# Values per tile of 116 tokens, moved to their rows by DMA, in a fused image-and-text transformer kernel

## What is computed

```python
h = concat([tokens(x), txt], axis=1)                 # (64, 87, 256)
y = layernorm(h)
q, k, v = split(y @ w_qkv.T)                         # 16 heads of 16
q, k = rope(norm_per_head(q)), rope(norm_per_head(k))
h = h + (softmax(q @ k.T / 4) @ v) @ w_proj.T + b_proj
z = layernorm(h)
h = h + z @ W_lin.T + b_lin + lora_of_the_top_2_of_8_experts(z)
```

## Time and profile before

| | |
|---|---|
| median of 3 runs | 793.22 us (786.54 to 795.9) |
| the profiled execution's own time | 798.07 us |
| its span, first to last instruction | 796.4 us |
| what lies around the span | 1.7 us |
| mean granted TensorE clock | 0.94 |
| busy: PE, PEld, DVE, ACT, POOL | 708.1, 564.9, 547.5, 408.2, 423.4 us |

### The profile page before, as it was taken

One profiled execution on the slowest core, in us unless ns is written; L12 is line 12 of the kernel. 1 busy time (PEld: TensorE's weight loads), 2 busy tenths in 40 slices (PEclk: granted clock), 3 DMA queues, 4 the chain that ended last, 5 costly groups with the idle time before them and its releaser, 6 DMA issues.

```text
span 796.4 us, 23804 instructions
## 1 busy us (share of the span) xinstructions
PE 708.1 (89%) x9335; PEld 564.9 (71%) x9335; DVE 547.5 (69%) x1208; ACT 408.2 (51%) x985; POOL 423.4 (53%) x450
## 2 busy tenths in 40 slices
PE   5998979987896388999899999999999999999974
PEld 4987757876673266887777777777777777877752
DVE  2377665873877556688677687887887887875641
ACT  4453423623433145666566556656557557666530
POOL 3577442652645726556447457566566566565211
PEclk9999969989897589999999999999999999999995
DMA  9940640704020121211221221222222222121100
GB/s 223 240 110 1 194 131 1 194 17 96 10 58 18 25 53 32 68 49 39 62 73 40 58 70 49 61 67 56 61 61 61 61 52 71 26 52 37 44 19 25
DMA packets 69524, 53.02 MB, mean 67 GB/s; under 512 B 36175, under 2 KB 68646, under 8 KB 69286
## 3 DMA queue, kind: packets, MB, share of 16 engines
q1 hardware_dynamic: 69414, 51.50, 25.9%
HBM read 33.69 MB, written 11.40 MB: 57 GB/s over the span
## 4 chain that ended last, share of the span: by engine, by line
PE 50%; DMA 13%; SPq 12%; DVE 11%; issue 5%; ACT 4%; POOL 4%; DVEq 0%; POOLq 0%; ACTq 0%
DMA out<-out_sb 8%; PE p_c L1305 8%; PE p_a L1305 7%; PE p_conv L764 6%; PE p_kv L764 6%; DMA xcols<-in_x_cols 5%; PE p_s L1366 4%; SPq L1060 4%; SPq L1061 4%; PE p_o L1375 3%; SPq L1050 2%; PE p_n L1383 2%; PE p_c L1423 2%; PE p_s L1348 2%; PE p_mm L764 2%
## 5 line engine op out<-in xcount | busy, mean ns | idle before, releaser
L1100 POOL TENSOR_TENSOR t<-t,ss_rs 116x512 f32<-116x512 f32 x48 | 51.0, 1062 | 152.8 <-ACT ss_rs L1149 152.8
L1243 DVE TENSOR_REDUCE mx<-p_s 87x16 bf16<-87x1392 f32 x64 | 102.2, 1597 | 8.9 <-PE p_s L1348 8.4
L1174 ACT ACTIVATE prT<-p_s 87x1392 f32<-87x1392 f32 x64 | 85.0, 1328 | 31.2 <-PE p_s L1366 31.2
L426 POOL TENSOR_TENSOR xs_lo<-xcols,xs_hi 120x585 fp32r<-120x585 f32 (+1 forms) x45 | 60.5, 1352 | 66.2 <-ACT xs_hi L489 66.2
L1096 POOL TENSOR_TENSOR t<-t 116x512 f32<-116x512 f32 x48 | 61.7, 1285 | 42.0 <-DVE t L1234 41.9
L1366 PE MATMUL p_s<-qr,kr 32*87 32x87 f32 x2048 | 68.6, 257 | 0.0
L1103 POOL TENSOR_TENSOR t<-t,tabs 116x512 f32<-116x512 f32 x48 | 61.1, 1273 | 1.5
L1305 PE MATMUL p_c<-w_f,yT 128*116 128x296 f32 x192 | 59.7, 436 | 1.7 <-ACT f L1199 0.6
L1366 PEld LDWEIGHTS p_s<-qr,kr 32*87 32x87 f32 x2048 | 60.1, 153 | 0.0
L1362 PE MATMUL p_s<-mxT,pick_row 32*87 32x87 bf16 x1024 | 55.7, 207 | 1.0 <-ACT mxT L1168 1.0
L1305 PE MATMUL p_c<-w_p,onT 128*116 128x256 f32 x192 | 54.3, 406 | 1.2 <-ACT yT L1193 0.9
(11 more groups left out here) (248 smaller groups left out, 1974.8 us busy)
## 6 DMA issues: line engine op xcount, KB each, us to landing
xcols<-in_x_cols SPq DMA_DIRECT2D x12, 822.7 KB, 11.8
h<-h_tokens SPq DMA_DIRECT2D x16, 348.0 KB
out<-out_sb SPq DMA_DIRECT2D x48, 116.0 KB
h_tokens<-in_txt SPq DMA_DIRECT2D x4, 1232.0 KB, 11.7
x<-in_txt_cols SPq DMA_DIRECT2D x32, 154.0 KB, 2.9
qr<-qkT SPq DMA_DIRECT2D x64, 58.0 KB, 2.0
kr<-qkT SPq DMA_DIRECT2D x64, 58.0 KB, 2.0
xcols<-in_x_cols SPq DMA_DIRECT2D x3, 759.4 KB, 13.5
```

The lines of the kernel that those rows point to most:

```text
L426: nc.gpsimd.tensor_tensor(xs.lo[:, n % XS_SLOTS, :, 0:M].bitcast(F32R), raw, xs.hi[:, n % XS_SLOTS, :, 0:M], ALU.subtract).then_inc(S['xs_ ...
L1100: link(nc.gpsimd.tensor_tensor(t4, t4, ss_rs[:, b].unsqueeze(2).broadcast_to([TP, 2 * HEADS, HD]), ALU.mult))
L1174: nc.scalar.activation(prT[:, k % 2], p_s[0:SEQ, :, 0:QUADS * SEQ], ACT.Exp, scale=HD ** -0.5).then_inc(S['s_exp'], 1)
L1243: nc.vector.reduce_max(mx[:, k % 2, :, 0:QUADS], p_s[0:SEQ, :, 0:QUADS * SP].rearrange("p j (a k) -> p j a k", k=SP)[:, :, :, 0:SEQ], AX_X ...
```

## The change

Values are made by tile: PE `v.0` makes tiles 0 and 1, `v.1` tile 2, each of 116 tokens (18 matmuls of 256 columns a group). ACT `v.0` to `v.2` scale by `a_rs`, which has the same tiling, and write `vt`. SP `values.0` (4 DMAs: tiles 0, 1) and `values.1` (2 DMAs: tile 2) carry the 6 pieces, 256 values a row, from `vt` to `vp`. `vp` is now `[token, 32, head]`, the weights' value columns are reordered on the host to suit, and `pv` reads its stationary operand with a step of 16 elements. SP `rstd` and `v_rs` go. `rstd_a` is issued earlier and waits for the evictions of the group before; `pv` waits for the DMAs' semaphores `v_in`. The fill of `twT`'s last row moves into `clear`. All five tables of group steps have new times and a new order; the period is 288.

```diff
--- before.py
+++ after.py
@@ -114,7 +114,7 @@
...
         loads = "wc_in cols_in wl_in wq_in rows_in wg_in wt_in x_in0 x_in1 x_in2 st_rows0 st_rows1 st_txt"
-        moves = "h_in0 h_in1 h_in2 h_in3 xT_in0 xT_in1 r_in0 r_in1 k_in00 k_in01 k_in10 k_in11"
+        moves = "h_in0 h_in1 h_in2 h_in3 xT_in0 xT_in1 v_in0 v_in1 k_in00 k_in01 k_in10 k_in11"
         self.loads = {n: ctx.enter_context(nc.semaphore("l_" + n)) for n in (loads + " " + moves).split()}
@@ -912,30 +912,32 @@
...
-GROUP_ACT = table("""xhi.0.-161 sq.0.-92 rstd_r.0.-40 sq.1.-21 rstd_a.0.-2 qkT.0.86 rstd_r.1.91 sq.2.110 qkT.1.158 rstd_r.2.187
-                qkT.2.242 mT.0.281 exp.0.297 v.0.312 v.1.316 mT.1.343 v.2.346 v.3.354 exp.1.360 oT.0.389
-                mT.2.414 oT.1.428 exp.2.433 oB.0.482 mT.3.499 oT.2.505 oB.1.510 exp.3.517 oB.2.572 oT.3.581
-                yT.0.639 oB.3.682 yT.1.713 rstd_c.0.744 ffn.0.751 ffn.1.783 yT.2.802 ffn.2.832 gate.0.898
-                twT.0.963""")
-GROUP_DVE = table("""stats.0.-405 stats.1.-329 stats.2.-179 eps.0.-86 rotate.0.-85 ss.0.-48 rotate.1.-14 ss.1.53 rotate.2.128
-                ss.2.179 max.0.254 max.1.321 max.2.382 norm.0.433 norm.1.454 max.3.475 norm.2.522 h2.0.592
-                stats_c.0.596 norm.3.637 h2.1.659 stats_c.1.663 h2.2.731 stats_c.2.736 logits.0.869 rank.0.915
-                weigh.0.933 out.0.985 out.1.989 out.2.1182""")
-GROUP_PE = table("""qk.0.-111 qk.1.-38 qkT.0.78 qk.2.92 qkT.1.151 qkT.2.231 peak.0.246 mT.0.276 scores.0.284 v.0.294 peak.1.314
-                pv.0.318 v.1.325 mT.1.339 scores.1.348 peak.2.375 oN.0.405 mT.2.409 pv.1.411 scores.2.420
-                oN.1.444 peak.3.459 oB.0.464 oB.1.492 mT.3.494 pv.2.495 scores.3.504 oN.2.514 oB.2.553
-                proj.0.556 pv.3.566 oN.3.629 yT.0.634 proj.1.646 oB.3.660 yT.1.706 proj.2.719 ffn.0.737
-                ffn.1.769 yT.2.791 ffn.2.812 twT.0.957 lora.0.973 lora.1.1175""")
-GROUP_POOL = table("""xc.0.-372 xlo.0.-130 add.0.-56 scale.0.-32 shift.0.-21 add.1.4 scale.1.99 shift.1.125 add.2.145 scale.2.194
-                shift.2.212 hb.0.406 hb.1.464 hb.2.513 base.0.883 above.0.891 base.1.976 base.2.1049""")
-GROUP_SP = table("""cols.0.-564 rows.0.-555 place.0.165 rstd.0.218 place.1.249 store.0.1164 store.1.1183 store.2.1368""")
-GROUP_PERIOD, GROUP_START = 289, 2100
+GROUP_ACT = table("""xhi.0.-161 rstd_a.0.-141 sq.0.-52 rstd_r.0.-1 sq.1.5 v.0.56 v.1.61 rstd_r.1.86 qkT.0.94
+                sq.2.125 qkT.1.184 v.2.209 rstd_r.2.223 qkT.2.268 mT.0.305 exp.0.322 oT.0.365 mT.1.371
+                exp.1.395 mT.2.440 oT.1.443 exp.2.458 mT.3.508 oB.0.530 oT.2.533 exp.3.538 oB.1.599
+                oT.3.623 oB.2.641 yT.0.697 oB.3.712 yT.1.719 rstd_c.0.789 ffn.0.805 ffn.1.839 yT.2.850
+                ffn.2.882 gate.0.955 twT.0.997""")
+GROUP_DVE = table("""stats.0.-397 stats.1.-348 stats.2.-342 eps.0.-316 rotate.0.-45 ss.0.-17 rotate.1.12 ss.1.53 rotate.2.146
+                ss.2.213 max.0.278 max.1.348 max.2.417 norm.0.459 max.3.484 norm.1.507 norm.2.551 h2.0.652
+                norm.3.661 h2.1.673 stats_c.0.691 stats_c.1.698 h2.2.760 stats_c.2.765 logits.0.892 rank.0.945
+                weigh.0.965 out.0.1025 out.1.1030 out.2.1200""")
+GROUP_PE = table("""qk.0.-70 qk.1.-13 v.0.39 qkT.0.81 qk.2.107 qkT.1.168 v.1.198 qkT.2.261 peak.0.265 mT.0.300 scores.0.309
+                peak.1.341 pv.0.355 mT.1.367 scores.1.382 peak.2.410 pv.1.418 oN.0.428 mT.2.435 scores.2.445
+                oN.1.469 peak.3.474 pv.2.479 mT.3.504 oB.0.520 scores.3.523 oN.2.544 oB.1.560 pv.3.589 oB.2.612
+                proj.0.633 oN.3.650 proj.1.661 yT.0.680 oB.3.702 yT.1.713 proj.2.748 ffn.0.781 ffn.1.820
+                yT.2.845 ffn.2.865 twT.0.992 lora.0.1012 lora.1.1182""")
+GROUP_POOL = table("""xc.0.-330 xlo.0.-130 add.0.-27 scale.0.6 shift.0.17 add.1.113 scale.1.126 shift.1.137 add.2.163
+                scale.2.230 shift.2.241 hb.0.385 hb.1.650 hb.2.657 base.0.893 above.0.918 base.1.953 base.2.968""")
+GROUP_SP = table("""cols.0.-564 rows.0.-500 values.0.96 place.0.191 place.1.275 values.1.323 store.0.1103 store.1.1107 store.2.1265""")
+GROUP_PERIOD, GROUP_START = 288, 2100
 H_SLOTS = 4
...
 K_COLS = [(0, 2 * TP), (2 * TP, GT)]
-SEGMENTS = [(b, t, max(SEQ * b, TP * t), min(SEQ * (b + 1), TP * (t + 1))) for b in range(GB) for t in range(TILES)
-            if max(SEQ * b, TP * t) < min(SEQ * (b + 1), TP * (t + 1))]
+V_TILES = [(0, 1), (2,)]
+SEGMENTS = [[(b, t, max(SEQ * b, TP * t), min(SEQ * (b + 1), TP * (t + 1))) for b in range(GB) for t in tiles
+             if max(SEQ * b, TP * t) < min(SEQ * (b + 1), TP * (t + 1))] for tiles in V_TILES]
+V_PARTS = [sorted({n for n, part in enumerate(SEGMENTS) for segment in part if segment[0] == b}) for b in range(GB)]
@@ -954,7 +956,6 @@
...
         epsb, a_ln, a_rs = sb("epsb", [TP, 2, TILES]), sb("a_ln", [TP, 2, TILES]), sb("a_rs", [TP, 2, TILES])
-        v_rs = sb("v_rs", [SEQ, 2, GB])
         x = sb("x", [P, 2, CC, GT])
@@ -966,7 +967,9 @@
...
         mxT = sb("mxT", [P, 2, SEQ], BF16)
-        vp = sb("vp", [SEQ, 2, GB, HEADS, 2 * HD])
+        vp = sb("vp", [SEQ, 2, GB, 2 * HD, HEADS])
+        vt = sb("vt", [TP, 2, TILES, C])
+        twT = sb("twT", [TILES * LR + 1, TP])
@@ -982,7 +985,6 @@
...
         tw = sb("tw", [TP, TILES, LR])
-        twT = sb("twT", [TILES * LR + 1, TP])
         out_sb = sb("out_sb", [TP, TILES, C])
@@ -1001,7 +1003,7 @@
...
         x_in = [consts.loads[f"xT_in{n}"] for n in range(2)]
-        r_in = [consts.loads[f"r_in{n}"] for n in range(2)]
+        v_in = [consts.loads[f"v_in{n}"] for n in range(2)]
         k_in = [[consts.loads[f"k_in{half}{n}"] for n in range(2)] for half in range(2)]
@@ -1043,12 +1045,13 @@
...
                                      ).then_inc(x_in[half], 16)
-                if name == 'rstd':
-                    wait(sp, S['a_rstd'], g + 1)
-                    wait(sp, S['v_out'], GB * (g - 1))
-                    for b, t, n0, n1 in SEGMENTS:
-                        sp.dma_start(v_rs[n0 - SEQ * b:n1 - SEQ * b, half, b:b + 1],
-                                     a_rs[n0 - TP * t:n1 - TP * t, half, t:t + 1]).then_inc(r_in[half], 16)
+                if name == 'values':
+                    sp.wait_ge(S['v_out'], TILES * g + V_TILES[k][-1] + 1)
+                    wait(sp, S['pv'], GB * (g - 1))
+                    wait(sp, v_in[k], 16 * len(SEGMENTS[k]) * g)
+                    for b, t, n0, n1 in SEGMENTS[k]:
+                        sp.dma_start(vp[n0 - SEQ * b:n1 - SEQ * b, half, b, 0:HD, :].rearrange("p d h -> p (d h)"),
+                                     vt[n0 - TP * t:n1 - TP * t, half, t]).then_inc(v_in[k], 16)
                 if name == 'place':
@@ -1072,7 +1075,8 @@
...
                     ready(nc.gpsimd.memset(part[:], 0.0))
-                ready(nc.gpsimd.memset(vp[:, :, :, :, HD:], 1.0))
+                ready(nc.gpsimd.memset(vp[:, :, :, HD:], 1.0))
+                ready(nc.gpsimd.memset(twT[TILES * LR:TILES * LR + 1], 1.0))
@@ -1106,7 +1110,6 @@
...
                         pool.wait_ge(W['agg'], STEPS)
-                        ready(nc.gpsimd.memset(twT[TILES * LR:TILES * LR + 1], 1.0))
                         pool.wait_ge(consts.S['rope_in'], 48)
@@ -1127,15 +1130,14 @@
...
                     wait(act, S['a_var'], 3 * g + 3)
-                    if g >= 2:
-                        act.wait_ge(r_in[half], 16 * len(SEGMENTS) * (g // 2))
+                    wait(act, S['v_out'], TILES * (g - 1))
                     link(nc.scalar.activation(a_ln[:, half], a_mv[:, half, :, 1], ACT.Ln, bias=eps5[0:TP, 0:1]))
...
                     wait(act, S['qk'], 3 * (g - 1))
-                    wait(act, S['v_mm'], 2 * (g - 1))
+                    wait(act, S['v_mm'], len(V_TILES) * (g - 1))
                     if g == 0:
@@ -1154,15 +1156,14 @@
...
                 if name == 'v':
-                    if g < 2 and k == 0:
-                        act.wait_ge(S['set_0'], VP_SET)
-                    wait(act, S['v_mm'], 2 * g + k // 2 + 1)
-                    if k == 0:
-                        act.wait_ge(r_in[half], 16 * len(SEGMENTS) * (g // 2 + 1))
-                    wait(act, S['pv'], GB * (g - 2) + k + 1)
-                    nc.scalar.activation(vp[0:SEQ, half, k, :, 0:HD],
-                                         p_a[0:SEQ, C * (k % 2):C * (k % 2 + 1)].rearrange("p (h d) -> p h d", d=HD),
-                                         ACT.Identity, scale=v_rs[:, half, k:k + 1]).then_inc(S['v_out'], 1)
+                    if g == 0 and k == 0:
+                        act.wait_ge(W['kv_mm'], CONVS)
+                    act.wait_ge(S['v_mm'], len(V_TILES) * g + k // 2 + 1)
+                    act.wait_ge(S['a_rstd'], g + 1)
+                    for n in range(2):
+                        wait(act, v_in[n], 16 * len(SEGMENTS[n]) * (g - 1))
+                    nc.scalar.activation(vt[:, half, k], p_a[0:TP, C * (k % 2):C * (k % 2 + 1)], ACT.Identity,
```

(25 more changed lines are left out.)

## The result

The changed kernel takes 763.4 us (median of 4 runs, 761.8 to 765.2), the kernel before 790.8 in the runs beside it (4 runs): ratio 0.965, 95% interval 0.958 to 0.972. So it is faster, by 27.4 us on the medians and 36.3 between the two profiled executions (798.1 and 761.8). The forecast was 777, its range 766 to 798: the direction was right, the gain larger than the whole range. The profiled execution before is slower than the medians of that kernel by 5 to 7 us (798.1 for 790.8 to 793.5), so gains read against its trace come out too large by about as much.

The account below looks back on a forecast made before the run. PE was taken to bound the kernel. From the profiled 798.1 us, -11.3 (values' matmuls), -6.3 (PE's waits) and +1 (start and end) gave 781.5, 16.6 less; on the median 793.2 that is 777 us, range 768 to 785, 766 to 798 with rivals.

Parts of the forecast that it names:

- The bound: Stretch 320 to 740 us, where groups follow one another: PE bounds, busy for 406.5 of 420 us.
- the values' matmuls: PE, each group: six of 24 matmuls go at 0.118 us, 0.71 us a group, 11.3 us over 16.
- the evictions: ACT: four of 0.468 us become three at the same price; ACT wins 7.5 us, nothing counted in the sum.
- The waits of PE: PE's waits for `out` (7.2 us) and `h2` (5.1 us) go; of 12.3 us half is counted, -6.3.
- The new holes: New gaps on PE in the group order, as around `p_s`; at worst 0.3 us a group beyond those that go, +5.
- Start and end: +1: Before and after the stream of groups: fills, early `v` steps and the end together +1 us, between -1 and +4.
- the longest landing seen: DMA landings: 8.66 us, of a store behind the `h` load, used as the worse case for the new transfers.
- The fills: Chain between the stages: `vp`'s fill keeps 2048 elements (1.80 us), `twT`'s (0.19 us) joins: +0.2.
- pv's stride: `pv`'s stationary operand read with a step of 64 bytes: load stays hidden, 0 us taken; other end 20 us.
- Rival 2: The strided load sets `pv`'s step, at four times a contiguous load: +20, 797 us; chance 0.13.
- SP's new transfers and `place.0`: SP's queue: issues of `values` about 0.6 us each, landings hidden before `pv`; `place.0` to `peak.0` keeps 1.3 us: 0 us.
- Rival 3: `place.0` lands late behind larger transfers, PE waits 2 us in each of 15 groups: 807 us; chance 0.08.

Follow-up runs that it names:

- rows_late_in_before: Kernel before with only the load of `h` moved from 555 to 500 units ahead of its group, for all groups: 771.3 us, ratio 0.974.
- stores_early_in_before: Kernel before with the stores of `out_sb` 164, 179 and 178 units earlier in SP's table, the load of `h` unmoved: 786.4 us, ratio 0.991.
- rows_late_group0: Kernel before with the load of `h` moved from 555 to 500 units ahead for group 0 alone: 780.6 us, ratio 0.982.
- sp_back_in_after: Kernel after with SP's loads of `h` (-555) and stores (1164, 1183, 1368) back at their old places: 775.9 us, ratio 0.979.
- order_only: Kernel before, values still made by image, with the kernel after's order of all steps, period 288 and `twT` fill: 780.5 us, ratio 0.985.
- values_in_old_order: Kernel after with the tables of before, only the values' steps placed early and the load of `h` at -500: 850.8 us, ratio 1.073.

## Why the prediction was wrong in size

**The bound, the values' matmuls, the evictions: right.** PE bounds, 96 matmuls a form, and the eviction's price is 472 ns for 468. From rows_late_in_before (29.7 us) to after (28.75, the mean of the middle periods) the period falls by 0.95 us; the forecast terms 0.71 (matmuls) and 0.4 (one `h2` wait), less 0.12 for the stride, make 0.99.

**"The waits of PE": the step that was half right.** Of the 12.3 us all but 1.2 went, where I counted 6.3. The new holes that I set against them did not come: the waits left are 1.8 us or less in all for each pair of engines, behind 695 us. Beyond them the waits for the store had a cost that I did not price: two of them halved the clock for 3.4 us each. The stream lost 11.1 us when the store waits of 7.2 us went (rows_late_in_before), 11.3 in stores_early_in_before. Matmuls for 15 periods (10.7), these 11.1 and the `h2` waits (5.1) make 26.9, less 1.8 for the stride 25.1, against 26.0 in the profiled executions; the forecast had 10.7 and 6.3, 17. On the medians, though, 16 to 17 us are left for the stream, the forecast's own number, and stores_early_in_before gives 7.2, not 11.3: how much more than 6.3 these waits cost depends on the execution, and they do not explain the miss.

**"Start and end: +1": the step that failed.** It measured -10.3 between the profiled executions, all of it at the start. With this term put right the sum comes out: 776.6 less 11.3 is 765.3, against medians of 763.4 and 765.8. The one table number behind it, tried alone, gave 13.0 us on the medians (rows_late_group0); put back in the kernel after, with the stores at their old places, it took away 12.6 us of the start and 10.1 to 12.6 of the medians, while the stream stayed as it was (sp_back_in_after). I had followed `rows` past the steps of its own group, and even took the 8.66 us of a store behind this load as a row, but not past the queue's entries of the window stage, where -555 and -500 lie on two sides of `x.1` and `x.2`. The prediction also calls 8.66 us "the longest landing seen"; the page before, part 6, has longer ones, and two of these three are the loads in question:

```profile
xcols<-in_x_cols SPq DMA_DIRECT2D x3, 759.4 KB, 13.5
```

The fills, on which I spent the step, did what was said.

**pv's stride: a term of the sum, mis-sized.** 0 us taken, about 1.8 measured in the trace (0.12 us a period), not separable in time. The forecast said that a load could take 2.7 times as long unseen; at 1.3 times, 32 matmuls already spread from 0.580 to 0.618 us. The load is largely hidden, but not wholly. Rival 2's 20 us is excluded: with the contiguous load the period falls by 0.12 us a group and no more. The Trainium skill's penalty for each new 16-byte line ("SBUF — State Buffer", Specifications) exists by this row; at 34 ns for 32 lines it is small.

**SP's new transfers and `place.0`: right in what they cost PE, wrong in their own size.** In the kernel after no wait for `vp<-vt` shows on PE, `kr` lands in 2.0 us as in the earlier trace rows. But the issues do not take 0.6 us each. In the kernel after the load stands right ahead of `values.0`, whose four issues take 7.10:

```profile
565.06 0.34 SPq L1039 DMA_DIRECT2D h<-h_tokens  x1
565.51 7.10 SPq L1053 DMA_DIRECT2D vp<-vt  x4
```

It is hidden because `pv` comes much later. The trace has no landings of `vp<-vt`, so "under 10 us" can't be read. Rival 3 did not happen, though its mechanism, a small transfer behind a large one, proved real in other places. VectorE waited for `h`, but only 3.5 us in two waits at the start (180 to 300 us):

```profile
DVE a_st L1220 <- DMA h<-h_tokens: 3.5, 2, 2.6
```

**Two sources of the gain.** On the medians, the load's one number gives 22.2 us and all the rest of the change 5 to 8. By the table of stretches, that rest wins 14.9 us in the stream (440.9 to 426.0) and gives back 4.2 at the start, beside the kernel that had only this number changed; the 2.3 us lost at the end are little more than the 1.7 by which two profiles of the kernel after differ there.

**Open:** why the start is 5 us longer with the new order and old values (order_only) than with the old order, beyond the 2.3 us of wait for `gw`, and why the end is; whether `v` among the steps that use `p_a` is what slows values_in_old_order; whether another placement would join the even 28.7 us period with the start at 272 us.

## What to carry to other kernels

When a large transfer moves in a queue, list what stands directly behind it at the old and at the new place, in every stage that the queue serves, the seam between two stages above all: that neighbour pays, not the transfer's own consumer. A wait on the bounding engine costs more than its length where it takes the clock with it (11 us of stream for 7 us of waits in the profiled executions here). And before a restructuring is costed or made, try its smallest part alone: one table entry held four fifths of this gain.
